# Attention and feed-forward block on one core: first-layer units issued by a list, ten in-place buffers, a third first-layer bank, softmax sums spread by a selection matmul, new slots

## The reference

```
x   = x + attention(layernorm(x, 1e-6))     # 8 heads of 16 channels, 768 x 768 scores per head
t   = x;  n = layernorm(t, 1e-5)
p   = top2(softmax(n @ Wg)), scaled to the sum 1     # two weights per token, 8 experts
out = t + sum over i in (0, 1) of
      ( sum over e of gelu((n * p_i) @ W1[e] + b1[e]) @ W2[e] + sum of b2 )
```

## Time and profile before

| | |
|---|---|
| median of three runs | 2684.5 us (2684.5 to 2685.81) |
| profiled execution | 2693.18 us, span of its instructions 2691.2 us |
| mean granted TensorE clock | 0.897 of 2.4 GHz |
| busy: PE, ACT, DVE, POOL | 87%, 62%, 51%, 39% of the span |
| one batch in the loop | 160.65 us |

### The profile page before, as it was taken

The page is one execution under the profiler, slowest core; times in us unless marked ns, Lnnn a source line. Parts: engine busy times, 40 slices in busy tenths (PEclk is TensorE's granted clock), DMA queues, the critical chain, the costliest instruction groups (busy, mean ns, idle before and its releaser), DMA issues.

```text
span 2691.2 us, 54396 instructions
## 1 busy us (share of the span) xinstructions
PE 2328.3 (87%) x17443; PEld 2071.1 (77%) x17443; DVE 1373.4 (51%) x3267; ACT 1661.6 (62%) x2760; POOL 1050.5 (39%) x1048
## 2 busy tenths in 40 slices
...
GB/s 47 75 38 45 8 30 26 14 45 7 34 19 33 26 9 47 10 27 26 21 38 7 42 11 32 27 10 45 10 28 26 28 30 8 49 7 30 26 10 7
DMA packets 70219, 71.22 MB, mean 26 GB/s; under 512 B 20462, under 2 KB 55242, under 8 KB 69962
## 3 DMA queue, kind: packets, MB, share of 16 engines
...
## 4 chain that ended last, share of the span: by engine, by line
PE 64%; issue 12%; DVE 11%; ACT 9%; SPq 2%; POOL 1%; DMA 0%; DVEq 0%; ACTq 0%; POOLq 0%
PE acc L858 18%; PE wide L784 9%; PE narrow L798 7%; PE zps L847 7%; PE zps L848 5%; PE zps L849 5%; ACT z L490 5%; PE wide L769 5%; DVE maxes L633 3%; DVE h L691 2%; PE wide L812 2%; PE wide L819 2%; PE wide L805 1%; ACT L490 1%; ACT h L519 1%
## 5 line engine op out<-in xcount | busy, mean ns | idle before, releaser
L431 POOL TENSOR_TENSOR hsum<-h 128x384 f32<-128x384 f32 x1024 | 1028.8, 1008 | 1553.6 <-ACT h L519 1533.3
L691 DVE TENSOR_TENSOR h<-zps,ratio_b 128x384 f32<-128x384 f32 x1024 | 561.0, 552 | 928.2 <-PE zps L849 925.9
L518 ACT ACTIVATE h<-zps,b_col 128x384 f32<-128x384 f32 x1024 | 593.5, 580 | 678.4 <-DVE h L691 659.2
L858 PE MATMUL acc<-w,hsum 128*128 128x128 f32 x6144 | 872.3, 279 | 1.5 <-DVE outt L700 1.2
L858 PEld LDWEIGHTS acc<-w,hsum 128*128 128x128 f32 x6144 | 857.1, 196 | 2.2 <-POOL hsum L431 1.7
L519 ACT ACTIVATE h<-h,b_col 128x384 f32<-128x384 f32 x1024 | 620.5, 606 | 0.0
L847 PE MATMUL zps<-x_hi,w_lo 128*128 128x384 f32 x1024 | 428.6, 419 | 88.2 <-DVE x_lo L670 47.9
L633 DVE TENSOR_REDUCE maxes<-wide 128x1 f32<-128x128 f32 (+5 forms) x768 | 437.3, 616 | 87.5 <-PE wide L769 83.8
L784 PE MATMUL wide<-stack 128*128 128x256 f32 (+3 forms) x1280 | 348.9, 432 | 108.2 <-ACT z L490 82.9
L784 PEld LDWEIGHTS wide<-stack 128*128 128x128 f32 x1280 | 264.1, 284 | 187.4 <-ACT z L490 159.0
L490 ACT ACTIVATE z<-wide 128x896 f32<-128x896 f32 (+2 forms) x384 | 343.5, 916 | 63.8 <-PE wide L784 54.9
...
## 6 DMA issues: line engine op xcount, KB each, us to landing
stack<-halves SPq DMA_DIRECT2D x384, 96.0 KB, 3.0
stack<-halves SPq DMA_DIRECT2D x384, 24.0 KB, 2.6
x_in<-in_x SPq DMA_DIRECT2D x136, 48.0 KB, 2.4
out_dram<-outt SPq DMA_DIRECT2D x256, 24.0 KB, 1.6
...
stack<-max_rows SPq DMA_DIRECT2D x128, 3.0 KB
stack<-max_rows SPq DMA_DIRECT2D x128, 1.5 KB
...
```

The costliest lines, as they stand in the source:

```text
L431: pool.tensor_tensor(hsum[:, m % NHS, :], h0[:, m % 2, :], h1[:, m % NH1, :], ALU.add).then_inc(hsum_ready, 1)
L518: act.activation(h0[:, m % 2, :], zps[m % 2][:, 0:CT], ACT.Gelu, bias=b1_col[:, j:j + 1]).then_inc(h0_ready, 1)
L691: vec.tensor_tensor(h1[:, m % NH1, :], zps[m % 2][:, 0:CT], ratio_b[:, c * CT:(c + 1) * CT], ALU.mult).then_inc(z1_ready, 1)
L858: ins = pe.matmul(acc[:, n * P:(n + 1) * P], hsum[:, k % NHS, n * P:(n + 1) * P], w2[:, j, :], start=(j == 0 and n == 0), stop=(j == UNITS ...
```

## The change

Five things change together.

1. **Units per slot.** In slot k not one but `FIRSTS[k]` units are issued (0 to 3), so that the first layer runs one to nine units ahead of the second. Slots 20 to 26, 42 to 44 and 58 to 60 issue none.
2. **Buffers.** `h1` is a ring of ten, POOL adds `h0` into it in place, and the second layer reads it there; `hsum` goes. The bank of `narrow` becomes a third `zps` bank, so PE waits for ACT's reading of the bank of about three units before. The rings' places are counted so that 64 units end where they began. `mix` (now one step of 768 columns and one copy) and `gate` use `wide`.
3. **Division.** `sums` goes. `divide` multiplies `mixed` by a 128x128 selection matrix, which gives each of the 32 rows of a head that head's row sum, and DVE inverts all 128x768 of them in PSUM before it multiplies.
4. **`project`** is done in two halves of 384 tokens, and `xn_ready` is raised per half after `weigh`.
5. **Slots.** Each step has a new slot; a slot with .5 puts the step behind the slot's second layer.

The lists:

```diff
-NHS = 4
+RING = 10
+FIRSTS = (1, 2, 0, 1, 0, 2, 1, 2, 3, 1, 0, 1, 3, 1, 1, 0, 1, 1, 1, 2, 0, 0, 0, 0, 0, 0, 0, 2, 3, 1, 2, 1,
+          1, 0, 2, 2, 1, 2, 0, 0, 1, 3, 0, 0, 0, 1, 1, 1, 1, 1, 1, 1, 1, 1, 0, 1, 3, 2, 0, 0, 0, 2, 1, 1)
+AT = {("stats", 0): -4.5, ("seed", 0): -4.5, ("root", 0): -2.0, ("scale", 0): -1.0, ("turn", 0): 0, ("query", 0): 0.5,
+      ("key", 0): 0.5, ("value", 0): 6.0, ("rows", 0): 16.5, ("mix", 0): 28.0, ("divide", 0): 32.5, ("rows", 1): 39.5,
+      ("mix", 1): 46.0, ("divide", 1): 48.0, ("project", 0): 49.5, ("project", 1): 51.0, ("stats", 1): 51.5, ("seed", 1): 53.0,
+      ("root", 1): 53.5, ("scale", 1): 55.0, ("turn", 1): 55.5, ("gate", 0): 57.0, ("weigh", 0): 59.0, ("split", 0): 60.0,
+      ("split", 1): 60.5}
+MAXIMA_AT = ((7, 7.5, 7.5, 8.5, 9.5, 10.0, 10.5, 12.0, 12.5, 13.5, 14.5, 15.0),
+             (26.5, 27.5, 28.0, 28.5, 28.5, 30.0, 31.5, 31.5, 35.0, 35.5, 37.0, 38.0))
+SCORES_AT = ((20.0, 21.5, 22.5, 23.0, 23.0, 23.5, 25.0, 26.0, 26.0, 26.0, 26.5, 26.5),
+             (43.0, 43.0, 43.0, 43.0, 43.5, 43.5, 43.5, 44.5, 44.5, 44.5, 44.5, 44.5))
...
-    def maxima(g, slots):
...
-    plan = [(-5, "stats", 0), (-5, "seed", 0), (-4, "root", (0, 0)), (-4, "root", (0, 1)), (-4, "root", (0, 2)),
-            (-3, "scale", (0, 0)), (-2, "scale", (0, 1)), (0, "turn", 0), (2, "query", 0), (2, "key", 0), (4, "value", 0)]
-    plan += [(4, "stack", (0, hh)) for hh in range(GH)]
-    plan += maxima(0, (8, 9, 10, 11, 12, 13, 14, 15, 16, 17, 18, 20)) + [(22, "rows", 0)]
-    for hh in range(GH):
-        plan += [(26, "scores", (0, hh, n)) for n in range(3)] + [(26, "stack", (1, hh))]
-    plan += [(27, "mix", (0, 0)), (28, "mix", (0, 1))]
-    late = [(30, "sums", 0), (32, "divide", 0)] + maxima(1, (31, 31, 32, 33, 34, 36, 36, 37, 38, 39, 39, 40))
-    plan += sorted(late, key=lambda step: step[0]) + [(41, "rows", 1)]
-    plan += [(44, "scores", (1, n // 3, n % 3)) for n in range(12)]
-    plan += [(44, "mix", (1, 0)), (45, "mix", (1, 1)), (46, "sums", 1), (47, "divide", 1), (49, "project", 0), (50, "load", 1)]
-    plan += [(50, "stats", 1), (51, "seed", 1), (51, "root", (1, 0)), (52, "root", (1, 1)), (52, "root", (1, 2)),
-             (54, "scale", (1, 0)), (54, "scale", (1, 1)), (56, "turn", 1), (57, "gate", 0), (58, "weigh", 0),
-             (60, "split", 0), (60, "split", 1)]
...
+    plan += parts("maxima", 0, MAXIMA_AT[0]) + [(AT["rows", 0], "rows", 0)]
+    for n, step in enumerate(parts("scores", 0, SCORES_AT[0])):
+        plan.append(step)
+        if n % 3 == 2:
+            plan.append((step[0], "stack", (1, n // 3)))
+    plan += [(AT["mix", g], "mix", g) for g in range(GROUPS)]
+    plan += [(AT["divide", g], "divide", g) for g in range(GROUPS)]
+    plan += parts("maxima", 1, MAXIMA_AT[1]) + [(AT["rows", 1], "rows", 1)] + parts("scores", 1, SCORES_AT[1])
...
-WIDE_STEPS = ("turn", "query", "key", "value", "maxima", "rows", "scores", "sums", "divide", "project", "split")
-NARROW_STEPS = ("mix", "gate")
+WIDE_STEPS = ("turn", "query", "key", "value", "maxima", "rows", "scores", "mix", "divide", "project", "gate", "split")
...
-NARROW = {(s, a): n for n, (s, a) in enumerate([(s, a) for _, s, a in PLAN if s in NARROW_STEPS])}
...
-NH1 = 4
+NH0 = 4
...
+def places(count):
+
+    turns = next([count] * n + [count - 1] * ((UNITS - count * n) // (count - 1)) for n in range(UNITS, -1, -1)
+                 if count * n <= UNITS and (UNITS - count * n) % (count - 1) == 0)
+    return [n for turn in turns for n in range(turn)]
...
+PLACE = places(RING)
+BACK = back(PLACE)
+BANKS = 3
+BANK = places(BANKS)
+BANK_BACK = back(BANK)
```

The order of a slot:

```diff
-                def steps(k, late):
+                def steps(lo, hi):
                     for r, start in ((following, 0), (ahead, UNITS)):
                         for slot, step, a in PLAN if r else ():
-                            if slot + start == k and (step in last) == late:
+                            if lo <= slot + start < hi:
                                 attention(r, step, a)
 
+                m = LAG
                 for k in range(UNITS):
-                    steps(k, False)
-                    if k + LAG < UNITS:
-                        unit(this, k + LAG)
-                    elif following:
-                        unit(following, k + LAG - UNITS)
+                    steps(k, k + 0.5)
+                    for _ in range(FIRSTS[k]):
+                        if m < UNITS:
+                            unit(this, m)
+                        elif following:
+                            unit(following, m - UNITS)
+                        m += 1
                     after(this, k)
-                    steps(k, True)
+                    steps(k + 0.5, k + 1)
```

On DVE:

```diff
-                elif step == "sums":
-                    vec.wait_ge(wide_filled[s], filled)
-                    vec.reciprocal(recip[:, :, :], w[:, 0:TILES * GH].rearrange("p (i g) -> p i g", g=GH)).then_inc(wide_free[s], 1)
...
+                    vec.reciprocal(w[:, 0:TOK], w[:, 0:TOK]).then_inc(inverted, 1)
+                    vec.wait_ge(inverted, r.at(GROUPS, a + 1))
                     vec.tensor_tensor(mixed_n[a][:, 0:TOK], mixed[:, :], w[:, 0:TOK], ALU.mult).then_inc(wide_free[s], 1)
                 elif step == "project":
+                    ts = slice(a * HT, (a + 1) * HT)
                     vec.wait_ge(wide_filled[s], filled)
-                    vec.tensor_tensor(xs[:, :, :], w[:, 0:TOK].rearrange("p (i c) -> p i c", c=C),
-                                      x_in[:, :, :], ALU.add).then_inc(wide_free[s], 1)
+                    vec.tensor_tensor(xs[:, ts, :], w[:, 0:CT].rearrange("p (i c) -> p i c", c=C),
+                                      x_in[:, ts, :], ALU.add).then_inc(wide_free[s], 1)
...
-                    ins.then_inc(xn_ready, 1)
+                        if i % HT == HT - 1:
+                            ins.then_inc(xn_ready, 1)
...
-                vec.wait_ge(hsum_ready, r.at(UNITS, m + 1))
-                vec.tensor_tensor(h1[:, m % NH1, :], zps[m % 2][:, 0:CT], ratio_b[:, c * CT:(c + 1) * CT],
+                vec.wait_ge(hsum_used, r.at(UNITS, m + 1 - BACK[m] + UNITS))
+                vec.tensor_tensor(h1[:, PLACE[m], :], zps[BANK[m]][:, 0:CT], ratio_b[:, c * CT:(c + 1) * CT],
                                   ALU.mult).then_inc(z1_ready, 1)
```

On PE:

```diff
-                elif step == "sums":
-
-                    pe.wait_ge(narrow_free, r.at(NPB, NARROW["mix", (a, 1)] + 1))
-                    for i in range(TILES):
-                        ins = pe.matmul(w[:, i * GH:(i + 1) * GH], mixed[:, i * P:(i + 1) * P], pick[:, :], start=True, stop=True)
...
+                    pe.wait_ge(*taken(r, "scores", (a, GH - 1, 2)))
...
+                                ins = pe.matmul(w[32 * hh:32 * hh + 32, start + q0:start + width], val[:, i, a * GH + hh, :],
+                                                z[:, hh, at:at + width - q0], start=(n == 0), stop=(n == len(tiles) - 1))
                     ins.then_inc(wide_filled[s], 1)
...
-                    pe.wait_ge(*taken(r, "sums", a))
-                    for i in range(TILES):
-                        for hh in range(GH):
-                            ins = pe.matmul(w[32 * hh:32 * hh + 32, i * P:(i + 1) * P], recip[:, i, hh:hh + 1].broadcast_to([P, 32]),
-                                            ident[:, :], start=True, stop=True)
-                    ins.then_inc(wide_filled[s], 1)
+                    pe.wait_ge(*taken(r, "mix", a))
+                    sums = pick[:, :, :].rearrange("p h d -> p (h d)")
+                    pe.matmul(w[:, 0:QCOLS], sums, mixed[:, 0:QCOLS], start=True, stop=True)
+                    pe.matmul(w[:, QCOLS:TOK], sums, mixed[:, QCOLS:TOK], start=True, stop=True).then_inc(wide_filled[s], 1)
...
-                    for i in range(TILES):
+                    for n in range(HT):
+                        i = a * HT + n
                         for g in range(GROUPS):
-                            ins = pe.matmul(w[:, i * P:(i + 1) * P], mixed_n[g][:, i * P:(i + 1) * P], wo_pad[:, g, :],
+                            ins = pe.matmul(w[:, n * P:(n + 1) * P], mixed_n[g][:, i * P:(i + 1) * P], wo_pad[:, g, :],
                                             start=(g == 0), stop=(g == GROUPS - 1))
```

More of the change, by code:

```diff
@@ L70, in attention_plan, with parts @@
-    plan += [(50, "stats", 1), (51, "seed", 1), (51, "root", (1, 0)), (52, "root", (1, 1)), (52, "root", (1, 2)),
-             (54, "scale", (1, 0)), (54, "scale", (1, 1)), (56, "turn", 1), (57, "gate", 0), (58, "weigh", 0),
-             (60, "split", 0), (60, "split", 1)]
-    return plan
+    def parts(step, g, slots):
+        return [(slot, step, (g, n // 3, n % 3)) for n, slot in enumerate(slots)]
+    plan = [(AT["stats", 0], "stats", 0), (AT["seed", 0], "seed", 0)]
+    plan += [(AT["root", 0], "root", (0, n)) for n in range(NEWTON)]
@@ new lines, in attention_plan @@
+    plan += [(AT["scale", 0], "scale", (0, n)) for n in range(2)]
```

(28 more changed lines are left out.)

98 lines of the change are left out of this document (42 added, 56 removed).

## The result

| | before | after |
|---|---|---|
| median, compared on one chip | 2684.9 us (4 runs) | 2734.7 us (4 runs, 2733.7 to 2737.7) |
| ratio | | 1.0187, 95% interval 1.0169 to 1.0205 |
| profiled execution, span | 2693.2, 2691.2 | 2737.7, 2735.8 |
| mean granted clock | 0.897 | 0.908 |

The change makes the kernel slower, by 50 us or 1.9%; 2660 was forecast. Page: span, busy engines, and the group of the long reciprocal.

The account below looks back on a forecast made before the run. PE bounds most stretches, ACT's Exps the scores, small DVE steps the batch change. Eight stretches summed to 158.6 us against 160.65: -30 over 15 iterations, +6 in the first batch, 2669 profiled, 2660 median; range 2570 to 2745.

Parts of the forecast that it names:

- The reciprocal: DVE's inversion of 768 elements in each divide: 5.1 us, from the slope between measured instructions of 6 and 24 elements.
- rival 1: Reciprocal dearer than 5.1 us or quite bare, at the first divide and the projection: 2708 us, slower; chance 0.14.
- A: Stretch from first turn to first scores: 38.0 us, between 37 and 39, from 42.9.
- C: Stretch from after the first mix to the second scores, with first divide: 31.6 us (28.5 to 34), from 29.4.
- G: Stretch from the projection to the next batch's first unit: 23.4 us (21.5 to 25.5), from 24.9.
- F: Projection stretch, waiting for reciprocal and multiplication: 11.4 us (10.1 to 13), PE standing 3.8 of it.
- B: Stretch of first scores and mix, where the gain was expected: 20.8 us (bounds 20 and 23), from 22.3.
- E: Stretch from after the second mix to the end of the second divide: 3.7 us, two pairs and the selection.
- H: Stretch from the next batch's first unit to the next turn: 8.7 us (8 to 9.8), from 9.8.
- D: Stretch of second scores and mix: 21.0 us (18.9 to 24), from 20.9, with the clock halving again.
- Rival 2: Clock halves behind gaps and stays down longer, at scores, divide, projection and turn: 5.5 us each iteration, 2742; chance 0.20.
- Rivals 3, 4 and 5: 3: lag covers more, 2585 us, 0.17. 4: reciprocal costs 0.95 us, 2529, 0.07. 5: lag and bank fail, 2684, 0.06.

Follow-up runs that it names:

- e2: Changed kernel with the old division put back (sums matmuls, inverse of 24 columns, matmuls that spread it): 2608.2 us, ratio 0.9705 to the kernel before.
- e4: Changed kernel plus filler matmuls nobody reads, ahead of the projection's first half and both turns, in the loop only: 2679.7 us, ratio 0.9973.
- e9: Changed kernel with the first group's reciprocal cut into two pieces of 384 columns, units' multiplications passing between: 2701.5 us, ratio 1.0055.
- e1: Changed kernel with the reciprocal run over only the first 24 of 768 columns: 2533.3 us, ratio 0.9426.
- e3: Kernel before with the new division alone (selection matmul, reciprocal over 768 columns): 2849.9 us, ratio 1.0607.

## Why the prediction was wrong

The direction failed; the time is inside the range. The balance: from the first unit to the last batch's `split` it was 2407.0 us before (191.0 to 2598.0) and is 2445.2 after (193.3 to 2638.5), +38 where -30 stood in the sum. That is 68 us too little. The first batch cost 2.3 and not 6, and the last batch, which was to stay, 4 more. 2669 + 68 - 4 + 4 = 2737, the profiled execution.

- **The reciprocal** was right: 5.1 from the slope, 4.97 measured. The Trainium skill ("VectorE: DVE Perf Modes", "First, the fixed hardware budget") gave 6.6, an estimate by my reading of its repeat count; the measurement decides against that reading. So rival 1 falls by its condition, though its sign came.
- **A, the largest miss (+2.2).** The step that failed is "38.0, between 37 and 39": it counts PE's pairs and attention steps, calls DVE "level" with them and puts every wait at nothing. A took 40.2, and in e2 40.0 to 40.5 whether its clock was 1.00, 0.71 or 0.58 behind the first turn. So the half clock there is not the missing term; at full clock the missing 1.8 us are PE's waits for ACT, DVE and the DMAs of `stack`. e4's 37.9 does not bear the count out: half of what it saves is added to H.
- **C (+1.3).** The gap was 3.81 us, 3.7 forecast; the mechanism (a unit's bank held behind DVE's queue) is in the brackets above, and e9 shows that its length in one piece matters. The term that failed is "some 0.8 for the clock behind it": the half clock lasted 5 to 6 us in eleven iterations and cost about 3, in three it lasted about 3 and C was 31.8 to 32.0, near the forecast. The work was 26.3 (e1), where I counted 27.1.
- **G (+1.1).** The projection to turn took 9.5, as forecast, with a gap of 3.82 (4). The 1.4 charged for the half clock and three units ahead of `gate` failed: turn to the first unit took 15.2 us in ten iterations, 14.3 in four and 13.1 at full clock (e4), so the units cost 0.6 and the half clock 1.9.
- **F (+0.8).** The gap ahead of the projection was 4.02 (3.8 forecast) and the two pairs ahead of it took 2.7 (2.4). "Some 1.3 for the halved clock" was nearly right: 1.4 in twelve iterations (the projection with its pair took 5.2 to 5.5 us, and 3.9 in e4), but 2.6 in two.
- **B (+0.4), E and H (0).** B was 21.1, but 22.7 in one iteration. H's 8.8 hides that it was 9.1 in ten iterations and 8.1 in four. **D (-1.3)** was better: its clock was 0.91, where I let it halve again.
- **The last batch (+4)** was one wait of 4.25 us of PE's second layer for DVE (`outt`), where the kernel before had 1.03. In the new slots the LayerNorm's roots and its scaling (2.44 us) stand ahead of `outt` in DVE's queue:

```profile
2646.78 2.44 DVE L642 TENSOR_SCALAR xn<-x_in,moments,ln_y 128x128 f32<-128x128 f32 x6
2649.14 0.54 DVE L715 TENSOR_TENSOR h<-zps,ratio_b 128x384 f32<-128x384 f32 x1
2649.61 0.54 DVE L724 TENSOR_TENSOR outt<-acc,res 128x384 f32<-128x384 f32 x1
```

The prediction said that over 161 us an iteration, with the reciprocal as taken, would mean the clock. That holds in part: of the 4.6 us by which the iteration missed, the half clock beyond what I had charged is about 2 in C and 1 in F and G together; A's 2.2 are waits, and D's -1.3 hides part of the sum. That e4's fillers take 4.7 from the iteration is a match by luck: they leave C's half clock in place, and take away what F and G had in the forecast already. Rival 2 (2742) came nearest and had C, F and G about right (+0.8, +0.8, +0.9 for +1.3, +0.8, +1.1) with its reason, a clock that stays down longer, but the +1.5 each in B and D never came, and A took their place. Rivals 3, 4 and 5 fall: C is over, not under, the forecast; the reciprocal is no 0.95; e2 shows the gain of lag and bank.

Against the kernel before the cause is another: the division, by e1, e2 and e3. A forecast with some stretches a little low (A, C, F, G by 5.4 us, of 159) was enough to turn the sign, because a gain of 6.9 us an iteration stood against a cost of 9.6 (in the windows of e2's quickest run; 5 against 8 by its median). The bounds of the range allowed 5 us each way, but the forecast's chance of 0.36 with a range of 2625 to 2680 did not.
